# A group norm, weight split and bidirectional convolutional GRU on one core: the head rebuilt, and the split of the image spread over the first blocks

## The chip, the cores and the metric

The kernel runs on 1 core of one Trainium2 chip. The metric is the device time of one execution in microseconds (us). Engines are named as in the profile: PE (TensorE), PEld (its weight loads), DVE (VectorE), ACT (ScalarE), POOL (GpSimd), SP (SyncE, which here only issues DMAs).

## The reference

```python
xs_h = x.transpose(2, 0, 1, 3)                      # x is the group norm of the input, 8x128x32x32
def step(h, xr):                                     # once per row (or column) of the image
    xi = xr.transpose(0, 2, 1).reshape(b * L, c)
    out = _gru_step(xi, h, wih, whh)                 # r, z, n = sigmoid, sigmoid, tanh; (1 - z) * n + z * h
    ctx = out.reshape(b, L, c).transpose(0, 2, 1)
    h_new = jnp.tanh(_conv1d(ctx, cw, cb)).transpose(0, 2, 1).reshape(b * L, c)
    return (h_new, ctx)
...
ctx_above = _direction(xs_h, wih_d, whh_d, cw_d, cb_d).transpose(1, 2, 0, 3)
ctx_below = _direction(xs_h[::-1], wih_u, whh_u, cw_u, cb_u)[::-1].transpose(1, 2, 0, 3)
ctx_left = _direction(xs_w[::-1], wih_r, whh_r, cw_r, cb_r)[::-1].transpose(1, 2, 3, 0)
out = jnp.einsum('bchw,oc->bohw', context_map, w_comb) + b_comb[None, :, None, None]
```

The input is normalised over 32 groups of 4 channels, three recurrences of 32 steps run over it (rows downwards, rows upwards, columns from the right), and the combination of their contexts is added to the input.

## The kernel before, in words

Products are made in float16 pairs: a value is split in a HI part (float16 of the scaled value) and a LO part (what is left), and each product is three matmuls: weights HI by data HI, weights LO by data HI, weights HI by data LO. The scales of the weights are powers of two from the largest column sum of each of seven sets.

**The three directions** k = 0, 1, 2 each take 32 steps s. `blocks` issues 33 x 3 blocks (t, j). Block (t, j) works on direction j at step t (`now`), on the next direction (`nxt`) and on the one before (`before`). In a block PE does the nine matmuls of a convolution, nine of the hidden products and nine of the input products, 256 columns each. ACT does, in this order: the tanh of the new value (`new_value`, L419), the tanh of a convolution (`hidden`, L424), the sigmoid of both gates of the next direction (`gates`, L407), the HI parts of the context and of the hidden state (L430, L435) and, where j is 2, the copy of the next image column (`column`, L402). DVE does `blend` (L600, L608), `reset_hidden` (L615), `context_lo` (L620), `tanh_argument` (L627), `hidden_lo` (L632) and `z_times_h` (L638). An engine takes its instructions in the order in which they are written. t = 0, 1 and 31, 32 are written out, and between them runs a hardware loop of 29 turns.

**The head**, before the first block. SP loads the weights of three directions, the combination's weights, and then the eight images. ACT sums the weights' magnitudes (L335); POOL takes the maximum over the partitions (`partition_all_reduce`, L285); DVE makes the scales; ACT scales the weights in place (L342) and rounds them (L348); POOL subtracts for the LO parts (`weights_lo`, L299). DVE takes the statistics of each image (L489, L493); PE averages them over the groups in three batches of images (L682, L685); POOL raises to the power -1/2 (L292). ACT and DVE write normalised copies of the images into halves of the context stores that are still free (L354, L527). The copies are split in HI and LO image by image: edge rows and last columns first (L370 to L373 on ACT, L307 on POOL, L536 on DVE), the rest (L360 and L544) partly ahead of and partly in the blocks (0, 0) to (1, 0):

```python
REST_HI_IN_BLOCK = {(0, 0): (4,), (0, 1): (5, 6), (0, 2): (7,)}
REST_LO_AHEAD = 3
REST_LO_IN_BLOCK = {(0, 0): (3,), (0, 1): (4, 5), (0, 2): (6,), (1, 0): (7,)}
```

PE runs 8 products into a bank that nobody reads (L825, `WARM_PRODUCTS`), waits for all edge splits and begins with `input_products(0, 0)`.

Of the kernel before, what the change touches and what calls it, by code (L numbers as in the profile page):

```python
# [18 lines left out]
STEPS = H  # L19
COLS = B * LINE  # L20
PAD = LINE + 2
SPACE = H * W
# [18 lines left out]
BATCHES = ((0, 3), (3, 7), (7, 8))  # L41
ACT_IMAGES = (0, 1, 3)
DVE_IMAGES = (2, 4, 5, 6, 7)
POOL_IMAGES = 2
EDGE = 4
LAST_COLS = 2
WHOLE_IMAGES = 3
REST_HI_IN_BLOCK = {(0, 0): (4,), (0, 1): (5, 6), (0, 2): (7,)}
REST_LO_AHEAD = 3
REST_LO_IN_BLOCK = {(0, 0): (3,), (0, 1): (4, 5), (0, 2): (6,), (1, 0): (7,)}  # L50
WARM_PRODUCTS = 8


def build(nc, x_d, w_d, bias_d, out_d):
# [4 lines left out]
    with ExitStack() as ctx:  # L59
# [27 lines left out]
        allsum = sb("allsum", [C, SETS], f32)  # L87
# [4 lines left out]
        group_avg = sb("group_avg", [C, C], f32)  # L92
        stats = sb("stats", [C, B, CHUNKS_B, 6], f32)
# [5 lines left out]
        inv_std = sb("inv_std", [C, B], f32)  # L99
# [4 lines left out]
        def two_images(k, part):  # L104
            lines = slice(STEPS // 2, STEPS) if k == 0 else slice(0, STEPS // 2)
            return ctx_store[k][:, part, lines, :, :].rearrange("p t b l -> p (t b l)")[:, 0:4 * SPACE] \
                .bitcast(f32).rearrange("p (i h w) -> p i h w", i=2, h=H)

        x_norm = [two_images(k, part)[:, i, :, :] for k in (0, 2) for part in range(2) for i in range(2)]
# [3 lines left out]
        magnitudes = ctx_store[2][:].rearrange("p a t b l -> p (a t b l)")[:, 0:2 * BLOCKS * C] \  # L113
            .bitcast(f32).rearrange("p (n c) -> p n c", n=BLOCKS)
# [13 lines left out]
        avg_bank = [conv_bank[0], conv_bank[1], n_bank[2]]  # L128
# [8 lines left out]
        aggr_done = sem("aggr_done")  # L137
        mean_avg = sem("mean_avg")
# [9 lines left out]
        x_lo_pool = sem("x_lo_pool")  # L148
        x_lo_dve = sem("x_lo_dve")
        rest_hi_done = sem("rest_hi_done")  # L150
        rest_lo_done = sem("rest_lo_done")
        x_col_done = sem("x_col_done")
        sum_done = sem("sum_done")
        allsum_done = sem("allsum_done")
        scale_done = sem("scale_done")
        w_scaled = sem("w_scaled")
# [37 lines left out]
        def blocks(eng, block):  # L194

            for t in (0, 1):
                for j in range(DIRS):
                    block(t, j)
            with eng.Fori(2, STEPS - 1) as t:
# [24 lines left out]
        def gate_scale(k):  # L224
            return descale[:, k:k + 1]
# [6 lines left out]
        def conv_scale(k):  # L232
            return descale[:, DIRS + k:DIRS + k + 1]
# [3 lines left out]
        def edge_rows(ap):  # L237
            return ap.rearrange("p (g r) w -> p g r w", r=EDGE)[:, 0:H // EDGE:H // EDGE - 1, :, :]

        def last_columns(ap):  # L240
            return ap[:, EDGE:H - EDGE, W - LAST_COLS:W]

        def rest(ap):
            return ap[:, EDGE:H - EDGE, 0:W - LAST_COLS]
# [4 lines left out]
        def _(sp):  # L249

            for k in list(range(DIRS)) + [COMB]:
# [16 lines left out]
        def _(pool):  # L268
# [11 lines left out]
                                    channel_multiplier=-1).then_inc(pool_built, 1)  # L280
            for k in range(DIRS):
                nc.gpsimd.memset(context[k][:, :, 0:PAD:PAD - 1], 0.0).then_inc(sides_zero, 1)

            pool.wait_ge(sum_done, SETS)
            nc.gpsimd.partition_all_reduce(allsum[:], abs_sum[:], C, bass.bass_isa.ReduceOp.max) \  # L285
                .then_inc(allsum_done, 1)

# [604 lines left out]
```

## Time and profile before

| | before |
|---|---|
| median of 3 runs | 366.3 us (366.17 to 366.49) |
| the profiled execution, its own time | 366.35 us |
| its span in the trace | 364.6 us |
| busy: PE, DVE, ACT, POOL | 324.1 (89%), 308.2 (85%), 275.0 (75%), 15.8 (4%) us |
| chain that ended last | PE 85%, ACT 5%, DVE 4%, issue 2%, DMA 2%, POOL 1% |
| instructions | 7973 |
| read and written in device memory | 6.16 MB, 4.19 MB |

The span is what the trace covers; 1.75 us of the execution's time lie around it. The chain is what led to the last instruction, followed backwards. Busy time counts overlapping instructions once.

### The profile page before, as it was taken

Reading aid. Unit: us, or ns where it says so; the run is one execution under the profiler, and the core shown is the slowest. Engines: PE = TensorE matmul, PEld = TensorE weight load, DVE = VectorE, ACT = ScalarE, POOL = GpSimd, SP = SyncE. Lnnn points to the kernel's source line nnn. Section 1 sums busy time; section 2 is a strip of 40 time slices with the busy share of each in tenths; the row PEclk is TensorE's granted clock in tenths of the full one; section 3 lists DMA queues with packets and bytes.
Section 4 is the critical chain, followed back from the end, with each engine's and each line's share of the span. In section 5 each row is a group of like instructions: output and inputs, shape, how many; then the busy total and the mean of one; then the engine's idle time right before and its main releaser. Section 6 shows DMA issues by size and latency. Waiting matters only on the chain.

```text
span 364.6 us, 7973 instructions
## 1 busy us (share of the span) xinstructions
PE 324.1 (89%) x2702; PEld 261.3 (72%) x2702; DVE 308.2 (85%) x766; ACT 275.0 (75%) x573; POOL 15.8 (4%) x26
## 2 busy tenths in 40 slices
PE   0002798999999999999999999999999999999995
PEld 0002477888888888888888888888888888873442
DVE  0659989999998899999999999999899888987875
ACT  6538897888888888888888888888888888867400
POOL 1056101000000000000000000000000000000000
PEclk9999899999999999999999999999999999999999
DMA  7900000000000000000000000000000000000433
GB/s 301 375 0 1 1 2 0 2 0 0 0 0 0 0 0 0 0 0 0 0 0 0 0 0 0 0 0 0 0 0 0 0 0 0 0 0 36 174 138 115
DMA packets 4182, 10.43 MB, mean 29 GB/s; under 512 B 592, under 2 KB 720, under 8 KB 4176
## 3 DMA queue, kind: packets, MB, share of 16 engines
q1 hardware_dynamic: 4176, 10.36, 7.4%
q8 instruction: 3, 0.05, 0.1%
q14 instruction: 3, 0.02, 0.0%
HBM read 6.16 MB, written 4.19 MB: 28 GB/s over the span
## 4 chain that ended last, share of the span: by engine, by line
PE 85%; ACT 5%; DVE 4%; issue 2%; DMA 2%; POOL 1%; SPq 0%; ACTq 0%
PE rz_bank L690 22%; PE conv_bank L690 17%; PE rz_bank L693 11%; PE n_bank L690 11%; PE conv_bank L693 8%; PE n_bank L693 5%; DMA ctx_store<-weights_dram 2%; ACT ctx_store L342 1%; PE rz_bank L776 1%; PE n_bank L776 1%; PE rz_bank L780 1%; PE n_bank L780 1%; PE n_bank L778 1%; PE rz_bank L778 1%; DVE stats L489 1%
## 5 line engine op out<-in xcount | busy, mean ns | idle before, releaser
L690 PE MATMUL conv_bank<-ctx_store,w_parts 128*128 (+1 forms) x558 | 108.9, 275 | 1.4 <-ACT ctx_store L430 0.9
L690 PE MATMUL rz_bank<-h_parts,w_parts 128*128 128x256 f16 x372 | 76.2, 273 | 0.1
L407 ACT ACTIVATE rz<-rz_bank,descale 128x512 f32<-128x512 f32 x96 | 65.9, 686 | 7.9 <-PE rz_bank L690 2.4
L419 ACT ACTIVATE nval<-npre 128x256 f32<-128x256 f32 x93 | 38.4, 413 | 40.5 <-DVE npre L627 40.5
L693 PE MATMUL conv_bank<-ctx_store,w_parts 128*128 (+1 forms) x279 | 67.2, 275 | 0.0
L690 PEld LDWEIGHTS conv_bank<-ctx_store,w_parts 128*128 128x128 f16 x558 | 54.3, 98 | 17.2 <-ACT ctx_store L430 6.6
L615 DVE SCALAR_TENSOR_TENSOR npre<-n_bank,descale,rz 128x256 f32<-128x256 f32 x93 | 45.0, 484 | 24.5 <-ACT rz L407 24.3
L690 PE MATMUL rz_bank<-x_rows,w_parts 128*128 (+1 forms) x256 | 52.8, 274 | 2.0 <-issue 2.0
L424 ACT ACTIVATE hval<-conv_bank,biases,descale 128x256 f32<-128x256 f32 x93 | 52.0, 560 | 0.0
L693 PE MATMUL rz_bank<-h_parts,w_parts 128*128 128x256 f16 x186 | 45.7, 273 | 0.0
L690 PE MATMUL n_bank<-h_parts,w_parts 128*128 128x256 f16 x186 | 45.6, 273 | 0.0
L627 DVE SCALAR_TENSOR_TENSOR npre<-n_bank,descale,npre 128x256 f32<-128x256 f32 x93 | 44.5, 478 | 0.0
L620 DVE SCALAR_TENSOR_TENSOR ctx_store<-context,ctx_store 128x272 f32 (+1 forms) x96 | 41.8, 436 | 0.6 <-ACT ctx_store L430 0.5
L608 DVE TENSOR_TENSOR context<-rz,nval 128x256 f32<-128x256 f32 x93 | 39.5, 425 | 3.2
L600 DVE SCALAR_TENSOR_TENSOR nval<-rz,nval 128x256 f32<-128x256 f32 x96 | 40.5, 422 | 1.3 <-ACT nval L419 0.7
L430 ACT ACTIVATE ctx_store<-context 128x272 f32 (+1 forms) x96 | 40.6, 423 | 1.0 <-DVE context L608 1.0
L690 PEld LDWEIGHTS rz_bank<-h_parts,w_parts 128*128 128x128 f16 x372 | 36.3, 98 | 5.4 <-DVE h_parts L632 0.4
L632 DVE SCALAR_TENSOR_TENSOR h_parts<-hval,h_parts 128x256 f16<-128x256 f32 x93 | 39.0, 420 | 0.4 <-ACT h_parts L435 0.4
L638 DVE TENSOR_TENSOR rz<-rz,hval 128x256 f32<-128x256 f32 x93 | 39.0, 420 | 0.0
L435 ACT ACTIVATE h_parts<-hval 128x256 f16<-128x256 f32 x93 | 37.5, 403 | 0.1
L402 ACT ACTIVATE x_col<-x_rows 128x512 f16 (+1 forms) x32 | 34.8, 1088 | 1.2 <-DVE x_rows L536 1.2
L693 PE MATMUL rz_bank<-x_rows,w_parts 128*128 (+1 forms) x128 | 35.0, 274 | 0.0
(110 smaller groups left out, 499.6 us busy)
## 6 DMA issues: line engine op xcount, KB each, us to landing
x<-x_dram SPq DMA_DIRECT2D x8, 512.0 KB, 9.3
out_dram<-x_rows SPq DMA_DIRECT2D x16, 256.0 KB, 2.0
ctx_store<-weights_dram SPq DMA_DIRECT2D x3, 576.0 KB, 5.1
ctx_store<-weights_dram SPq DMA_DIRECT2D x1, 192.0 KB, 6.1
biases<-biases_dram SPq DMA_DIRECT2D x1, 2.0 KB, 11.6
```

The costliest lines, as they stand in the source:

```text
L407: nc.scalar.activation(rz[k][:].rearrange("p g c -> p (g c)"), rz_bank[k][:], ACT.Sigmoid, scale=gate_scale(k)).then_inc(sig_done[k], 1)
L424: nc.scalar.activation(hval[k][:], conv_bank[k % 2][:, 0:COLS], ACT.Tanh, bias=biases[:, k:k + 1], scale=conv_scale(k)).then_inc(h_done[k], 1)
L430: nc.scalar.activation(context_lines(k, s, HI), context[k][:].rearrange("p b l -> p (b l)"), ACT.Copy, scale=ACT_SCALE).then_inc(ctx_hi_do ...
L600: nc.vector.scalar_tensor_tensor(nval[k][:], z, 1.0, nval[k][:], ALU.subtract, ALU.mult).then_inc(zn_done[k], 1)
L608: nc.vector.tensor_tensor(out=context[k][:, :, 1:1 + LINE], in0=lines(zh), in1=lines(nval[k][:]), op=ALU.subtract).then_inc(ctx_done[k], 1)
L615: nc.vector.scalar_tensor_tensor(npre[k][:], n_bank[k][:, COLS:2 * COLS], gate_scale(k), rz[k][:, 0, :], ALU.mult, ALU.mult).then_inc(rh_d ...
L620: nc.vector.scalar_tensor_tensor(context_lines(k, s, LO), context[k][:].rearrange("p b l -> p (b l)"), ACT_SCALE, context_lines(k, s, HI), ...
L627: nc.vector.scalar_tensor_tensor(npre[k][:], n_bank[k][:, 0:COLS], gate_scale(k), npre[k][:], ALU.mult, ALU.add).then_inc(npre_done[k], 1)
L632: nc.vector.scalar_tensor_tensor(h_parts[k][:, LO, :], hval[k][:], ACT_SCALE, h_parts[k][:, HI, :], ALU.mult, ALU.subtract).then_inc(h_lo_ ...
L638: nc.vector.tensor_tensor(out=rz[k][:, 0, :], in0=rz[k][:, 1, :], in1=hval[k][:], op=ALU.mult)
L690: last = nc.tensor.matmul(out, w_block(HI, k, n), parts(hi_or_lo), start=start, stop=stop and hi_or_lo == LO, skip_group_check=True)
L693: last = nc.tensor.matmul(out, w_block(LO, k, n), parts(HI), start=False, stop=False, skip_group_check=True)
```

## The change

- SP loads the first direction's weights, then the eight images, then the other weights. Once all 19 splits of the image are made (`SPLITS`), it loads the eight images a second time, since they are now normalised in place and the sum at the end needs the input; ACT waits for that before the last additions.
- The maxima of the weight sums are taken by PE: one matmul turns the sums onto a few partitions (L729), DVE reduces, and a second matmul spreads the result (L735). It is done for the first two sets alone and later for the other five.
- ACT takes the mean and the variance of images 2 and 5 (L384 to L392), DVE those of six images. One average over the groups serves all images. POOL does the power once, and no other work beside the setting up of constants.
- ACT rounds and scales weights in one instruction (L398); DVE makes their LO parts in one (L580). It is done in ten units of three 128x128 blocks (`UNITS`), four of them ahead of the blocks.
- The image is normalised in its own place in three pieces: edge rows (2 + 2), a strip of 4 columns, and the core of 28x28. Core pieces stand in blocks (0, 1), (0, 2) and (1, 0), three on ACT, five on DVE.
- The split in HI (L412, ACT) and LO (L571, DVE) takes a strip of all eight images at once: two strips ahead of the blocks, 17 in blocks (0, 0) to (9, 2). `WAIT_SPLITS` names the blocks in which PE waits for every split of the blocks before.
- Blocks t = 0 to 10 are written out; the loop has 20 turns.
- PE has 12, 4, 4 and 6 products that nobody reads, between the small matmuls of the head.

```diff
+SPLIT_IN_BLOCK = {
+    (0, 0): LAST_COLS,
+    (1, 0): Cells((2, 4), (0, W - 4)),
+    (1, 1): Cells((H - 4, H - 2), (0, W - 4)),
+    (1, 2): Cells((4, 6), (0, W - 4)),
+    (2, 0): Cells((8, H - 8), (W - 8, W - 4)),
+    (2, 1): Cells((H - 6, H - 4), (0, W - 4)),
+    (2, 2): Cells((6, 8), (0, W - 4)),
+    (3, 0): Cells((H - 8, H - 6), (0, W - 4)),
+    (4, 0): Cells((8, 10), (0, W - 8)),
+    (4, 2): Cells((H - 10, H - 8), (0, W - 8)),
+    (5, 1): Cells((12, H - 12), (W - 12, W - 8)),
+    (6, 0): Cells((10, 12), (0, W - 8)),
+    (6, 2): Cells((H - 12, H - 10), (0, W - 8)),
+    (7, 2): Cells((12, 14), (0, W - 12)),
+    (8, 1): Cells((14, 16), (0, W - 12)),
+    (9, 0): Cells((16, 18), (0, W - 12)),
+    (9, 2): Cells((18, 20), (0, W - 12)),
+}
+WAIT_SPLITS = ((0, 0), (1, 2), (2, 0), (3, 2), (4, 0), (7, 2), (8, 0), (10, 1))
...
+def splits_before(t, j):
+
+    return 2 + sum(block < (t, j) for block in SPLIT_BLOCKS)
...
+UNITS_IN_BLOCK = {(0, 0): ("in 2", "conv 1"), (0, 1): ("rec 1",), (0, 2): ("conv 2",), (1, 0): ("rec 2",),
+                  (3, 1): ("comb",)}
+CORE_ON_ACT = {(0, 1): (5,), (0, 2): (6,), (1, 0): (7,)}
+CORE_ON_DVE = {(0, 1): (0, 1), (0, 2): (2, 3), (1, 0): (4,)}
...
+            load_weights(0)
             for b in range(B):
                 sp.dma_start(x32[:, b, :, :], x_d[b, :, :, :]).then_inc(x_loaded[b], 16)
+            for k in (1, 2, COMB):
+                load_weights(k)
             sp.dma_start(biases[:], bias_d).then_inc(bias_loaded, 16)
+
+            sp.wait_ge(x_lo_done, SPLITS)
+            for b in range(B):
+                sp.dma_start(x32[:, b, :, :], x_d[b, :, :, :]).then_inc(x_loaded[b], 16)
...
+            def image_moments(b):
+
+                i = ACT_IMAGES.index(b)
+                act.wait_ge(x_loaded[b], 16)
+                moment(nc.scalar.activation(summed[:, 2 * i, :, :], x32[:, b, :, :], ACT.Identity,
+                                            accum_out=image_sum[:, i:i + 1]))
...
+                moment(nc.scalar.activation(summed[:, 2 * i + 1, :, :], x32[:, b, :, :], ACT.Square,
+                                            bias=minus_mean[:, i:i + 1], accum_out=square_sum[:, i:i + 1]))
...
+            def x_hi(cells, normed):
+
+                act.wait_ge(x_normed, normed * (B - len(ACT_NORMED)))
+                act.wait_ge(x_normed_act, normed * len(ACT_NORMED))
+                nc.scalar.activation(all_images(x_rows[:, HI, :, :, :], cells),
+                                     x32[:, :, cells.rows, cells.cols], ACT.Copy).then_inc(x_hi_done, 1)
+
+            magnitude_sums(0)
+            image_moments(ACT_IMAGES[0])
+            for unit in range(3):
+                weights_hi(unit)
+            image_moments(ACT_IMAGES[1])
+            for k in (1, 2, COMB):
+                magnitude_sums(k)
+            for b in ACT_NORMED:
+                normalise(b, edges)
+            x_hi(FIRST_ROWS, 1)
+            x_hi(LAST_ROWS, 1)
+            for b in ACT_NORMED:
+                normalise(b, strip)
+            weights_hi(UNITS.index("in 1"))
...
+                    for unit in UNITS_IN_BLOCK.get((t, j), ()):
+                        weights_hi(UNITS.index(unit))
+                    for b in CORE_ON_ACT.get((t, j), ()):
+                        normalise(b, core)
+                    if (t, j) in SPLIT_IN_BLOCK:
+                        x_hi(SPLIT_IN_BLOCK[t, j], 2 if t == 0 else 3)
...
+                if isinstance(t, int) and (t, j) == (0, 0):
+                    act.wait_ge(x_lo_done, splits_before(0, 1))
+                    column(0)
...
+            def x_lo(cells):
+
+                lo_count[0] += 1
+                dve.wait_ge(x_hi_done, lo_count[0])
+                nc.vector.tensor_tensor(out=all_images(x_rows[:, LO, :, :, :], cells),
+                                        in0=x32[:, :, cells.rows, cells.cols],
+                                        in1=all_images(x_rows[:, HI, :, :, :], cells),
+                                        op=ALU.subtract).then_inc(x_lo_done, 1)
...
+            image_stats(0)
+            sets_peak(0)
+            image_stats(1)
+            weight_scales(0)
+            image_stats(3)
+            image_stats(4)
+            weights_lo(0)
+            weights_lo(1)
+            image_stats(6)
+            image_stats(7)
+            spread()
+            weights_lo(2)
+            variance()
+            shift()
+            for b in dve_normed:
+                normalise(b, edges)
+            sets_peak(1)
+            x_lo(FIRST_ROWS)
+            weight_scales(1)
+            x_lo(LAST_ROWS)
+            for b in dve_normed:
+                normalise(b, strip)
+            weights_lo(UNITS.index("in 1"))
...
+            pe.wait_ge(pool_built, 6)
+            turn_sums(0)
+            spread_peaks(0)
+            pe.wait_ge(w_hi_done, 2)
+            warm(FRONT_WARM)
+            pe.wait_ge(aggr_done, B - len(ACT_IMAGES))
+            pe.wait_ge(act_stats, 2 * len(ACT_IMAGES))
+            nc.tensor.matmul(avg_bank[:, 0:B], group_avg[:], meanvar[:, :, 0],
+                             start=True, stop=True).then_inc(mean_avg, 1)
+            warm(CHAIN_WARM)
+            pe.wait_ge(spread_done, 1)
+            nc.tensor.matmul(var_bank[:, 0:B], group_avg[:], dev[:],
+                             start=True, stop=True).then_inc(var_avg, 1)
+            warm(CHAIN_WARM)
+            turn_sums(1)
+            spread_peaks(1)
+            warm(LAST_WARM)
...
                 k, s = lagged(t, j, -1)
+                if isinstance(t, int) and t < UNROLLED and (t, j) in WAIT_SPLITS:
+
+                    pe.wait_ge(x_lo_done, splits_before(t, j))
```

ACT in the blocks (0, 0) and (0, 1), before. Each row is an instruction with its tiles and the semaphores it waits for; `x_rows<-ctx_store` is a rest of an image being rounded.

```order
43 L407 ACTIVATE rz<-rz_bank,descale 128x512 [waits rz_ready_1]
44 L360 ACTIVATE x_rows<-ctx_store 128x24x30
45 L430 ACTIVATE ctx_store<-context 128x272 [waits ctx_done_0]
46 L415 ACTIVATE nval<-n_bank,descale 128x256 [waits n_ready_1]
47 L407 ACTIVATE rz<-rz_bank,descale 128x512 [waits rz_ready_2]
48 L360 ACTIVATE x_rows<-ctx_store 128x24x30 x2
```

The same place now: the first column (`x_col`) is no longer copied ahead of the blocks.

```order
27 L440 ACTIVATE rz_1<-rz_bank_1,descale 128x512 [waits rz_ready_1]
28 L398 ACTIVATE w_parts<-ctx_store_1,w_scale 128x384 [waits scale_done] x2
29 L412 ACTIVATE x_rows<-x32 128x8x28x4 [waits x_normed_act,x_normed]
30 L463 ACTIVATE ctx_store_0<-context_0 128x272 [waits ctx_done_0]
31 L435 ACTIVATE x_col<-x_rows 128x512 [waits x_lo_done]
32 L448 ACTIVATE nval_1<-n_bank_1,descale 128x256 [waits n_ready_1]
33 L440 ACTIVATE rz_2<-rz_bank_2,descale 128x512 [waits rz_ready_2]
34 L398 ACTIVATE w_parts<-ctx_store_1,w_scale 128x384 [waits scale_done]
35 L404 ACTIVATE x32<-x32,x_shift,x_scale 128x28x28 [waits x_factor]
```

Behind the sigmoid of direction 1 there stand now two units of weights and the split of the last columns; the column's copy waits for DVE's half of that split.

DVE in block (1, 1), before, where the block holds no extra work:

```order
92 L600 SCALAR_TENSOR_TENSOR nval<-rz,nval 128x256 [waits n_done_1]
93 L608 TENSOR_TENSOR context<-rz,nval 128x8x32 [waits zn_done_1]
94 L615 SCALAR_TENSOR_TENSOR npre<-n_bank,descale,rz 128x256 [waits n_ready_2,sig_done_2]
95 L620 SCALAR_TENSOR_TENSOR ctx_store<-context,ctx_store 128x272 [waits ctx_hi_done_1]
96 L627 SCALAR_TENSOR_TENSOR npre<-n_bank,descale,npre 128x256 [waits rh_done_2]
```

The same block now:

```order
74 L642 SCALAR_TENSOR_TENSOR nval_1<-rz_1,nval_1 128x256 [waits n_done_1]
75 L650 TENSOR_TENSOR context_1<-rz_1,nval_1 128x8x32 [waits zn_done_1]
76 L657 SCALAR_TENSOR_TENSOR npre_2<-n_bank_2,descale,rz_2 128x256 [waits n_ready_2,sig_done_2]
77 L571 TENSOR_TENSOR x_rows<-x32,x_rows 128x8x2x28 [waits x_hi_done]
78 L662 SCALAR_TENSOR_TENSOR ctx_store_1<-context_1,ctx_store_1 128x272 [waits ctx_hi_done_1]
79 L669 SCALAR_TENSOR_TENSOR npre_2<-n_bank_2,descale,npre_2 128x256 [waits rh_done_2]
```

A split stands between the reset gate's product and the LO part of the context, and all that follows on DVE is queued behind it.

PE at the input products of block (1, 2), now (before, the same row waited for `rest_lo_done`):

```order
115 L765 MATMUL rz_bank<-h_parts,w_parts 128x256
116 L765 MATMUL n_bank<-h_parts,w_parts 128x256
117 L768 MATMUL n_bank<-h_parts,w_parts 128x256
118 L765 MATMUL n_bank<-h_parts,w_parts 128x256
119 L765 MATMUL rz_bank<-x_rows,w_parts 128x256 [waits sig_done_0,x_lo_done]
```

The input products of direction 0 wait here for the split of the block before; blocks (2, 0) and (8, 0) have such a row too.

## Rows read from the trace of the kernel before

**Rows 1.** First line of the page.

```profile
span 364.6 us, 7973 instructions
```

**Rows 2.** Timeline of the head: start, us, engine, line, operation, tiles [idle before <-releaser].

```profile
4.89 0.84 ACT L335 ACTIVATE ctx_store<-ctx_store 128x768 f32<-128x768 f32 x1 [2.61 <-DMA ctx_store<-weights_dram]
...
15.43 1.23 DVE L489 BATCH_NORM_STATS2 stats<-x 128x6 f32<-128x512 f32 x2
...
34.14 1.12 POOL L292 TENSOR_TENSOR inv_std<-gvar,minus_half 128x4 f32<-128x4 f32 x1 [0.61 <-DVE gvar L511]
...
35.96 3.50 PE L825 MATMUL rz_bank<-w_parts 128*128 128x512 f16 x8
...
41.42 0.27 PE L690 MATMUL rz_bank<-x_rows,w_parts 128*128 128x256 f16 x1 [1.96 <-issue]
```

**Rows 3.** Windows: us, PE, PEld, DVE, ACT, POOL busy (x), PEclk, DMA share, GB/s.

```profile
14.00:16.00 2.00, 0.00 (x0) 0.00 (x0) 1.97 (x6) 1.89 (x3) 0.00 (x0) 1.00 1.05 420
...
43.00:44.00 1.00, 1.00 (x6) 0.75 (x5) 1.00 (x2) 0.87 (x3) 0.00 (x0) 0.50 0.00 0
...
120.00:129.00 9.00, 9.00 (x84) 7.79 (x82) 8.12 (x22) 7.55 (x17) 0.00 (x0) 1.00 0.00 0
```

**Rows 4.** Timeline of ACT: the sigmoids of the gates in the first blocks.

```profile
43.66 0.69 ACT L407 ACTIVATE rz<-rz_bank,descale 128x512 f32<-128x512 f32 x1
...
45.62 0.68 ACT L407 ACTIVATE rz<-rz_bank,descale 128x512 f32<-128x512 f32 x1
...
49.92 0.69 ACT L407 ACTIVATE rz<-rz_bank,descale 128x512 f32<-128x512 f32 x1 [0.66 <-PE rz_bank L690]
...
54.19 0.67 ACT L407 ACTIVATE rz<-rz_bank,descale 128x512 f32<-128x512 f32 x1
...
58.08 0.69 ACT L407 ACTIVATE rz<-rz_bank,descale 128x512 f32<-128x512 f32 x1 [0.24 <-PE rz_bank L690]
...
61.11 0.69 ACT L407 ACTIVATE rz<-rz_bank,descale 128x512 f32<-128x512 f32 x1
...
64.08 0.69 ACT L407 ACTIVATE rz<-rz_bank,descale 128x512 f32<-128x512 f32 x1
```

**Rows 5.** Timeline of ACT in a block with a column, in the loop.

```profile
123.83 0.69 ACT L407 ACTIVATE rz<-rz_bank,descale 128x512 f32<-128x512 f32 x1
124.41 0.42 ACT L430 ACTIVATE ctx_store<-context 128x272 f32 x1
124.73 0.41 ACT L435 ACTIVATE h_parts<-hval 128x256 f16<-128x256 f32 x1
125.04 1.09 ACT L402 ACTIVATE x_col<-x_rows 128x512 f16 x1
126.04 0.40 ACT L419 ACTIVATE nval<-npre 128x256 f32<-128x256 f32 x1
126.34 0.54 ACT L424 ACTIVATE hval<-conv_bank,biases,descale 128x256 f32<-128x256 f32 x1
```

**Rows 6.** Timeline of DVE in the same block.

```profile
124.55 0.48 DVE L615 SCALAR_TENSOR_TENSOR npre<-n_bank,descale,rz 128x256 f32<-128x256 f32 x1 [0.28 <-ACT rz L407]
124.95 0.43 DVE L620 SCALAR_TENSOR_TENSOR ctx_store<-context,ctx_store 128x272 f32 x1
125.30 0.48 DVE L627 SCALAR_TENSOR_TENSOR npre<-n_bank,descale,npre 128x256 f32<-128x256 f32 x1
```

**Rows 7.** Groups of 0 to 58 us, shapes apart: count | busy, mean ns | idle before.

```profile
L544 DVE TENSOR_TENSOR x_rows<-ctx_store,x_rows 128x720 f16<-128x720 f32 x8 | 7.0, 900 | 0.0
...
L360 ACT ACTIVATE x_rows<-ctx_store 128x720 f16<-128x720 f32 x5 | 3.9, 797 | 0.0
...
L354 ACT ACTIVATE ctx_store<-x,x_shift,x_scale 128x1024 f32<-128x1024 f32 x3 | 3.7, 1236 | 7.9 <-DVE x_shift L523 7.9
L342 ACT ACTIVATE ctx_store<-ctx_store,w_scale 128x384 f32<-128x384 f32 x4 | 2.4, 600 | 0.0
...
L536 DVE TENSOR_TENSOR x_rows<-ctx_store,x_rows 128x256 f16<-128x256 f32 x6 | 2.5, 417 | 0.0
```

More of the change, by code:

```diff
@@ L92, in build @@
         group_avg = sb("group_avg", [C, C], f32)
+        unit_diag = sb("unit_diag", [C, C], f32)
+        ones = sb("ones", [SETS, C], f32)
+        peak = [sb(f"peak_{n}", [SETS, 1], f32) for n in range(2)]
+        peak_diag = [sb(f"peak_diag_{n}", [SETS, SETS], f32) for n in range(2)]
+        image_sum = sb("image_sum", [C, len(ACT_IMAGES)], f32)
+        minus_mean = sb("minus_mean", [C, len(ACT_IMAGES)], f32)
+        square_sum = sb("square_sum", [C, len(ACT_IMAGES)], f32)
         stats = sb("stats", [C, B, CHUNKS_B, 6], f32)
@@ L194, in blocks @@
         def blocks(eng, block):
-            for t in (0, 1):
+            for t in range(UNROLLED):
                 for j in range(DIRS):
                     block(t, j)
-            with eng.Fori(2, STEPS - 1) as t:
+            with eng.Fori(UNROLLED, STEPS - 1) as t:
                 for j in range(DIRS):
@@ L232, in conv_scale, with edges, strip, core @@
         def conv_scale(k):
[L233 to L244, printed above, removed]
+            return descale[:, 2 * k + 1:2 * k + 2]
+        def edges(ap):
+            return ap.rearrange("p (g r) w -> p g (r w)", r=2)[:, 0:H // 2:H // 2 - 1, :]
+        def strip(ap):
+            return ap[:, LAST_COLS.rows, LAST_COLS.cols]
+        def core(ap):
+            return ap[:, LAST_COLS.rows, 0:LAST_COLS.cols.start]
+        def all_images(ap, cells):
+            return ap[:, cells.rows, :, cells.cols].rearrange("p h b w -> p b h w")
+        def unit_blocks(unit):
+            kind, *k = UNITS[unit].split()
+            if kind == "comb":
+                return COMB_SET, 0, DIRS
+            k = int(k[0])
+            first = DIRS + k * DIR_BLOCKS + GATES * ("in", "rec", "conv").index(kind)
+            return 2 * k + (kind == "conv"), first, first + GATES
+        def merged(ap):
+            return ap.rearrange("p n c -> p (n c)")
         block = ctx.enter_context(nc.Block())
@@ L249, in _, with load_weights @@
         def _(sp):
-            for k in list(range(DIRS)) + [COMB]:
+            def load_weights(k):
                 lo, hi = (DIRS + k * DIR_BLOCKS, DIRS + (k + 1) * DIR_BLOCKS) if k != COMB else (0, DIRS)
@@ L560, in _ @@
+            dve_normed = [b for b in range(B) if b not in ACT_NORMED]
             image_stats(0)
-            weight_scales()
+            sets_peak(0)
             image_stats(1)
-            image_stats(2)
-            spread(0)
+            weight_scales(0)
             image_stats(3)
-            variance(0)
             image_stats(4)
-            factor(0)
-            shift(0)
-            image_stats(5)
+            weights_lo(0)
+            weights_lo(1)
             image_stats(6)
-            normalise(2)
@@ L649, in steps @@
                 if exists(now[1]):
[L650 to L651 removed]
+                    if isinstance(t, int):
+                        for unit in UNITS_IN_BLOCK.get((t, j), ()):
+                            weights_lo(UNITS.index(unit))
+                        for b in CORE_ON_DVE.get((t, j), ()):
+                            normalise(b, core)
+                        if (t, j) in SPLIT_IN_BLOCK:
+                            x_lo(SPLIT_IN_BLOCK[t, j])
                     context_lo(*now)
@@ new lines, in spread_peaks, with warm @@
+            def spread_peaks(n):
+                first, end = SET_GROUPS[n]
+                pe.wait_ge(peak_done, n + 1)
+                nc.tensor.matmul(peak_bank[n][:, C:C + end - first], ones[0:end - first, :],
+                                 peak_diag[n][0:end - first, 0:end - first], start=True, stop=True) \
+                    .then_inc(peak_spread, 1)
+            def warm(products):
+                for _ in range(products):
+                    nc.tensor.matmul(rz_bank[2][:], w_block(HI, 0, 0),
+                                     merged(w_parts[:, HI, DIRS:DIRS + OUT_COLS // C, :]),
+                                     start=True, stop=True, skip_group_check=True)
```

318 lines of the change are left out of this document (124 added, 194 removed).

## The prediction

> **What bounds the kernel now.** I read three things in this order: the windows, to see what a block in the loop costs and which engine fills it; the timeline of the head, to see when the first real matmul can run; and the sigmoids of the gates on ACT as milestones, since each block has exactly one.
>
> In the loop PE is busy 9.00 us of 9.00 and makes three blocks in that time [rows 3]. A block's 27 matmuls therefore last 2.98 us, and ACT and DVE must fit in between. They do so narrowly. From one sigmoid (call its start 0) ACT goes 0.58 to the context's HI part, 0.90, 1.21 to the column, 2.21 to the tanh, 2.51 to the next tanh [rows 5], and the next sigmoid can start 0.46 later: at 2.97, exactly PE's period. Without the column it is bound by DVE instead: the reset product at 0.72, context LO at 1.12, tanh argument at 1.47, done at 1.95 [rows 6], then 0.33 and 0.46 on ACT: 2.77, so 0.2 us of slack. **The loop has nearly no room for extra work.** The span runs 41.42 us without a real matmul [rows 2], and the first blocks, which hold the rest of the split, take 4.30, 4.27 and 3.89 us instead of 3 (differences of neighbours from 45.62 to 58.08, [rows 4]). What the change can win is in that head; what it can lose is in the blocks.
>
> **The new head, step by step.** Weights 0 land at 4.89 as before [rows 2]. An image of 0.52 MB takes 1.25 us at 420 GB/s [rows 3]: image 0 lands at about 6.1, image 2 at 8.7, image 7 at 14.9, the last weights at 18.2.
> - DVE: six images of statistics, 1.45 each (two halves 1.23 [rows 2] and some 0.2 for the aggregation), 8.7; scales and peaks of two sets about 1.2; two LO units at 0.55 each (384 elements, between 0.42 and 0.90 [rows 7]). From 6.1 that ends at 17.2.
> - ACT: image 2 from 8.7, two passes of about 1.3 and three tiny instructions, 3.2; three units at 0.51 (0.60 less the overlap [rows 7]); image 5, 3.2: 16.7. The sums of the other weights last until 20.1, behind the chain.
> - Chain: mean matmul 0.6 to 17.9, three small DVE steps to 18.45, warm products, second average to 19.2, power 1.12 [rows 2] to 20.6, shift 20.85, edges of five images 21.7, HI of the first rows 22.3, LO 23.0. PE then still has six warm products: 1.3 us at the full clock, 2.6 at half. The eight products of before took 3.50 us [rows 2], 0.43 for 512 columns, which is the 1.2 GHz level. So the first real matmul comes at 23.9 to 25.1 instead of 41.42.
> - Direction 1 must wait for the unit "in 1", the last item of DVE's list, at 25.9. Its sigmoid comes at 26.95, against 43.66 [rows 4]: **minus 16.7**. POOL's subtractions and the three-batch chain vanish here, with no successor on the path.
>
> **The first blocks, sigmoid to sigmoid.** Prices: a split of 448 elements costs ACT 0.57 (between 272 elements at 0.42 [rows 5] and 720 at 0.797 [rows 7]) and DVE 0.62 (between 0.417 and 0.900 [rows 7]), 0.53 as a step in DVE's queue. A core of 784 costs ACT 0.97 (below 1.236 for 1024 [rows 7]) and DVE 0.62 as a step, my estimate; bounds 0.42 and 0.90.
> - (0, 0): two units 1.02, last columns 0.93, then DVE's LO 1.0, then the column 1.09, which is now ahead of direction 2's first product, then 1.05 on PE: 0.58+1.02+0.93+1.07+1.1+1.05 = 5.75, against 1.96: **plus 3.8**.
> - (0, 1): ACT adds 1.48 where two rests took 1.4 before: 4.5, **plus 0.2**. (0, 2): adds 1.48 where 0.7 stood: 5.05, **plus 0.8**.
> - (1, 0): unit, core and split are in series, and the split on ACT must wait for DVE's last core, which waits for ACT's unit: LO ends at 3.63, then 0.35+0.51+0.33+0.46: 5.3 against 3.89, **plus 1.4**.
> - PE blocks (1, 2) and (2, 0) wait for the split of the block just before, though the line they read was ready earlier. That split ends at 1.16+0.60 = 1.76; then nine input products 0.97, nine of the convolution 1.0, and the first of the hidden ones 0.68: 4.45. Against 3.03 and 2.97 [rows 4] that is **plus 1.4 and plus 1.5**.
>
> **The spread splits.** With a split in it, a block's chain is: ACT to 1.13, DVE starts at 1.16, 0.53, then 0.35+0.51+0.33+0.46 = 3.34 instead of 2.97, plus 0.37. With a column ACT needs 3.44, plus 0.47. In a lone split PE keeps part of its lead, and it costs what the context's HI part is late, 0.13 to 0.23. Four splits in a run, (2, 0) to (3, 0), make 1.7, the unit "comb" 0.43, the eight singles 0.07 to 0.22 each 1.3; block (8, 0) waits as (2, 0) does, 1.2. **Plus 4.6** in all. Below, a split can cost nothing (all slack in the next block), above, both its steps in full, 1.0.
>
> **The loop.** Nine turns fewer. Two neighbouring periods are 3.03 and 2.97 [rows 4], so a turn's end costs 0.06: **minus 0.5**. The Trainium skill (Runtime: NRT & Kernel Launch, Instruction fetch mechanics) says that a taken branch leaves the sequential prefetch and can stall on a fetch; the trace shows only those 0.06 us, and by a full stall a turn the gain would be larger.
>
> **The clock.** PE's granted clock was 0.50 in 43 to 44 us [rows 3], after PE had stood idle 1.96 us before its first real product [rows 2], and only six matmuls started in that microsecond, where the loop starts 84 in 9 us [rows 3]. In the new start-up PE idles 4.6 us behind block (0, 0), so I expect the same once or twice and take **plus 1.2** (bounds 0 and 7.2, below).
>
> **The tail.** The images loaded again, 4.2 MB, take 10 us at 420 GB/s [rows 3] from about 115 us on and are needed at 325: nothing. If that cover went, ACT would wait those 10 us at the end. The tail is the same.
>
> Sum: -16.7+3.8+0.2+0.8+1.4+1.4+1.5+4.6-0.5+1.2 = **-2.3 us**. The profiled execution took 366.35 us with a span of 364.6 [rows 1], and stands 0.05 above the median: 364.05, so **364.0 us**. Most of 16.7 us of gain is given back later.
>
> **Rivals.**
> - **The clock stays low (slower).** At the 1.2 GHz level 27 products take 5.75 us. Were it low through the start-up, the three middle blocks would grow by 1.25, 0.7 and 0.45, and the two that wait (24 products 5.1, behind the split's 1.76) by 2.4 each: 7.2, less the 1.2 counted: 370.0 us. It decides once the low stretch costs more than 3.5 us. For it: PE will be busy only 60% of a start-up block. Against: at the low clock PE is filled, and after such a stretch the clock came back, since the loop runs 84 products in 9 us [rows 3]. The Trainium skill (TensorE: Matmul & The Clock Gate, The HAM clock gate) has throttled as the default state and activity as what releases it, which makes this rival possible by rule.
> - **Splits cost both steps in full (slower).** 14 extras at 0.8 instead of a mean of 0.24: plus 7.8, 371.8 us. For it: DVE has 0.9 us free in 9 [rows 3]. Against: the chain above has room.
> - **The head is not as short.** The one average waits for the last of eight images and for both ACT images; a hidden wait among the many semaphore hops, or direction 1's unit, may cost 3 us: 367 us.
> - **The blocks absorb it (faster still).** DVE is ahead in the waited-for splits (minus 3.5), lone splits free (minus 1.2), no clock loss (minus 1.2): 358.1 us.
>
> **How the numbers follow.** Forecast, within 2 us of 364.0: 0.55. Absorbed: 0.18. Head longer: 0.12. Clock: 0.09. Full price: 0.06. A measurement of this kernel tells 0.2%, 0.7 us, from no change. Faster: 0.53 from the forecast, 0.18 from absorbed and 0.01 from the long head, 0.72. Same: 0.02 from the forecast, 0.04 from the long head, 0.06. Slower: 0.07 from the long head and both dear cases, 0.22. The range leaves out the two dear cases and the end of the cheap one: 358.5 to 368.5 us.
>
> **What would show it.** The first input product at 24 to 25 us; gaps between the sigmoids of 5.7, 4.5, 5.0, 5.3, 4.4, 4.4; PE in the windows from 55 to 100 us busy less than 9 of 9, with periods of 3.2 to 3.5 in blocks with a split and 4.2 before (8, 0); the granted clock at 0.5 somewhere between 25 and 40 us. I am wrong if the first product comes after 28 us, if blocks with a split have a period of 2.98, or if the low clock lasts over 8 us.

## The result and the profile after

The changed kernel took 369.2 us (median of 20 runs, 367.4 to 371.0), the kernel before 367.1 us in the same comparison (20 runs, 366.1 to 368.2). The ratio is 1.0054, with a 95% interval of 1.0034 to 1.0074: **0.5% slower**, where 364.0 us and faster was forecast. Half of the changed kernel's runs lie between 367.4 and 368.4 us and half between 370.0 and 371.0, so that the median stands in the gap, where no run is; what parts them comes below. The profiled execution is of the lower half (367.5 us). In it the change costs 1.2 us of span against [rows 1].

The head of the page after, and its rows of busy time and granted clock:

```profile
span 365.8 us, 7776 instructions
...
PE 330.9 (90%) x2720; PEld 260.7 (71%) x2720; DVE 309.7 (85%) x772; ACT 277.8 (76%) x590; POOL 4.2 (1%) x16
...
PEclk9988999999999999999999999999999999999999
```

There are 197 instructions fewer, and the span is no shorter for it. Of 40 slices two have a clock digit of 8 (18 to 37 us). The timeline of the head after answers to [rows 2]:

```profile
5.41 0.84 ACT L377 ACTIVATE ctx_store<-ctx_store 128x768 f32<-128x768 f32 x1 [3.11 <-DMA ctx_store<-weights_dram]
...
23.17 2.74 PE L741 MATMUL rz_bank<-w_parts 128*128 128x512 f16 x6
25.70 0.42 PE L765 MATMUL rz_bank<-x_rows,w_parts 128*128 128x256 f16 x1
```

The first real matmul starts at 25.70 us instead of 41.42. **The head is 15.7 us shorter, nearly all that was claimed for it.** The gates' sigmoids on ACT, the milestones of [rows 4], show where it goes:

```profile
27.91 0.69 ACT L440 ACTIVATE rz<-rz_bank,descale 128x512 f32<-128x512 f32 x1
33.94 0.69 ACT L440 ACTIVATE rz<-rz_bank,descale 128x512 f32<-128x512 f32 x1 [0.92 <-PE rz_bank L765]
39.27 0.69 ACT L440 ACTIVATE rz<-rz_bank,descale 128x512 f32<-128x512 f32 x1 [1.40 <-PE rz_bank L765]
44.26 0.68 ACT L440 ACTIVATE rz<-rz_bank,descale 128x512 f32<-128x512 f32 x1
49.56 0.69 ACT L440 ACTIVATE rz<-rz_bank,descale 128x512 f32<-128x512 f32 x1
54.28 0.69 ACT L440 ACTIVATE rz<-rz_bank,descale 128x512 f32<-128x512 f32 x1
59.00 0.69 ACT L440 ACTIVATE rz<-rz_bank,descale 128x512 f32<-128x512 f32 x1
62.54 0.69 ACT L440 ACTIVATE rz<-rz_bank,descale 128x512 f32<-128x512 f32 x1
```

Call direction 1's first sigmoid number 1; number 3t+j+1 is the one that PE's block (t, j) leads to, and ACT's block (t, j) runs from there to the next. Number 1 is 15.75 us earlier than before (27.91 against 43.66, [rows 4]), number 7 only 5.08 (59.00 against 64.08), number 24 still 1.20 (113.67 against 114.87). Number 25 is 0.34 late, behind PE's wait in block (8, 0), and from number 32 on the changed kernel is 1.1 to 1.2 us late, until the end. The forecast had minus 16.7, then minus 6.4, then minus 2.3.

The two periods of 4.72 (to 54.28 and 59.00) are the waits for a split just before, as forecast. The timelines of DVE and PE after show the second:

```profile
55.46 0.62 DVE L571 TENSOR_TENSOR x_rows<-x,x_rows 128x448 f16<-128x448 f32 x1
...
56.15 0.28 PE L765 MATMUL rz_bank<-x_rows,w_parts 128*128 128x256 f16 x1 [1.58 <-DVE x_rows L571]
```

PE stood 1.58 us for the LO half of rows that its block does not read. A block with one split in the loop's steady part is the next loss. ACT's and DVE's timelines after, block (4, 0), where a split of 384 elements stands alone:

```profile
79.25 0.68 ACT L440 ACTIVATE rz<-rz_bank,descale 128x512 f32<-128x512 f32 x1
79.83 0.52 ACT L412 ACTIVATE x_rows<-x 128x384 f16<-128x384 f32 x1
80.24 0.42 ACT L463 ACTIVATE ctx_store<-context 128x272 f16<-128x272 f32 x1
...
82.58 0.69 ACT L440 ACTIVATE rz<-rz_bank,descale 128x512 f32<-128x512 f32 x1
```

```profile
79.96 0.48 DVE L657 SCALAR_TENSOR_TENSOR npre<-n_bank,descale,rz 128x256 f32<-128x256 f32 x1
80.38 0.56 DVE L571 TENSOR_TENSOR x_rows<-x,x_rows 128x384 f16<-128x384 f32 x1
80.85 0.44 DVE L662 SCALAR_TENSOR_TENSOR ctx_store<-context,ctx_store 128x272 f16<-128x272 f32 x1
81.20 0.48 DVE L669 SCALAR_TENSOR_TENSOR npre<-n_bank,descale,npre 128x256 f32<-128x256 f32 x1
81.60 0.41 DVE L674 SCALAR_TENSOR_TENSOR h_parts<-hval,h_parts 128x256 f16<-128x256 f32 x1
```

The period is 3.33 us instead of 2.97. PE's timeline has one gap in it:

```profile
80.22 0.27 PE L765 MATMUL n_bank<-x_col,w_parts 128*128 128x256 f16 x1
80.72 0.28 PE L765 MATMUL conv_bank<-ctx_store,w_parts 128*128 128x256 f16 x1 [0.22 <-ACT ctx_store L463]
...
82.17 0.38 PE L765 MATMUL rz_bank<-h_parts,w_parts 128*128 128x256 f16 x2
```

Neighbouring products start 0.11 us apart, so the convolution's turn was at 80.33, and it starts 0.39 late, when the context's HI part (L463) is done. That part stands behind ACT's half of the split, a step of 0.41 (79.83 to 80.24). In the kernel before, it was done at 121.86 and the convolution started at 121.97, in its turn: after a hop of 0.06 as here (80.66 to 80.72) PE had some 0.05 us of lead, and nearly the whole step reaches the period. Behind the gap PE runs without another one to the products that release the sigmoid at 82.58.

DVE is close behind. Its half takes 0.47 us of its queue (80.38 to 80.85), and everything behind it is late by that: the context's LO part, and `hidden_lo` (L674), which the last two products of the gates read. It ends at 82.01 and they start at 82.17, so here they don't wait. In the kernel before, it ended 2.28 us after the start of the sigmoid before it (120.86) and they started 2.55 after it; now it ends 2.76 after it: had ACT's half cost nothing, this path would still have made the block about 0.27 longer (an estimate from these times and the hop of 0.06).

PE was busy 8.71 of 9 us between 120 and 129, against 9.00 before [rows 3], since splits still stand there. The images' second load, whose cover the forecast named, cost nothing; PE is full while it runs:

```profile
140.00:144.00 4.00, 4.00 (x38) 3.47 (x37) 3.44 (x9) 3.23 (x8) 0.00 (x0) 1.00 1.02 398
```

### The profile page after: what moved, and what is told of

The parts are those of the page before. It is cut to its first block, busy times and chain, and to the rows that moved or that the text cites. A ratio compares the mean times of both kernels' runs of the same rounds, so it can differ in the third digit from the quotient of the medians.

```text
span 365.8 us, 7776 instructions
## 1 busy us (share of the span) xinstructions
PE 330.9 (90%) x2720; PEld 260.7 (71%) x2720; DVE 309.7 (85%) x772; ACT 277.8 (76%) x590; POOL 4.2 (1%) x16
## 4 chain that ended last, share of the span: by engine, by line
PE 75%; ACT 12%; issue 6%; DVE 5%; POOL 1%; POOLq 0%; ACTq 0%
PE rz_bank L765 19%; PE conv_bank L765 16%; PE rz_bank L768 9%; PE n_bank L765 9%; PE conv_bank L768 8%; PE n_bank L768 4%; ACT rz L440 3%; ACT x_col L435 2%; ACT x_rows L412 2%; DVE x_rows L571 1%; ACT hval L457 1%; ACT ctx_store L463 1%; PE rz_bank L851 1%; ACT nval L452 1%; DVE npre L657 1%
## 5 line engine op out<-in xcount | busy, mean ns | idle before, releaser
L463 ACT ACTIVATE ctx_store<-context 128x272 f32 (+1 forms) x96 | 40.5, 422 | 1.0 <-DVE context L650 1.0
L674 DVE SCALAR_TENSOR_TENSOR h_parts<-hval,h_parts 128x256 f16<-128x256 f32 x93 | 38.5, 414 | 0.2 <-ACT h_parts L468 0.2
```

The source lines that it names most:

```text
L463: nc.scalar.activation(context_lines(k, s, HI), context[k][:].rearrange("p b l -> p (b l)"), ACT.Copy, scale=ACT_SCALE).then_inc(ctx_hi_do ...
```

## Experiments

Every comparison is with the kernel before, on the same chip. Its median there was 367.7 us. A period is read from one profiled execution of each kernel.

**Wait only for what is read.** In the three places PE waits for one split fewer.

```diff
-pe.wait_ge(x_lo_done, splits_before(t, j))
+pe.wait_ge(x_lo_done, splits_before(t, j) - ((t, j) in ((1, 2), (2, 0), (8, 0))))
```

> Edit: in blocks (1, 2), (2, 0) and (8, 0) PE waits for one split fewer, so not for the split of the block just before, which the products there do not read. Theory A (the wait is on the path): the periods before the three following sigmoids, 4.72, 4.72 and 4.51 us in the changed kernel, fall to what ACT and DVE need with a split, 3.4 to 3.5; the kernel gets 3.5 to 4 us faster than the changed one, about 365.3 us. Theory B (ACT and DVE bound these blocks anyway): less than 1 us.

Measured: 364.25 us (6 runs, 363.0 to 367.0), ratio 0.9921, interval 0.9892 to 0.9951. ACT's timeline in this kernel:

```profile
52.81 0.69 ACT L440 ACTIVATE rz<-rz_bank,descale 128x512 f32<-128x512 f32 x1 [0.71 <-PE rz_bank L765]
56.23 0.69 ACT L440 ACTIVATE rz<-rz_bank,descale 128x512 f32<-128x512 f32 x1
59.65 0.69 ACT L440 ACTIVATE rz<-rz_bank,descale 128x512 f32<-128x512 f32 x1
```

The two periods fall from 4.72 to 3.42, that of (8, 0) from 4.51 to 3.32: 3.8 us together. **The over-strict waits alone turn the sign of the change**: without them it is faster than the kernel before. Two of the six runs, the profiled one with them, are near 367 us and four at 363.0 to 364.6.

**Idle products against the low clock.** On the changed kernel, ten products with no use behind direction 1's first input products, to keep PE from standing idle in block (0, 0).

```diff
                 if exists(s):
                     input_products(k, s)
+                if isinstance(t, int) and (t, j) == (0, 0):
+                    warm(10)
```

> Edit: ten products of 512 columns that nobody reads behind the input products of direction 1, in PE's idle stretch of 4.6 us before the first column. Theory A (the low clock behind the stretch costs time): granted clock stays at the 2.4 GHz level from 28 to 38 us, the next two periods, 6.03 and 5.33 us, fall by 0.3 and 0.7 us, in all 1 us faster than the changed kernel, and its runs scatter less than 367.4 to 371. Theory B (the clock falls elsewhere, or falls harmlessly): within 0.3 us, same scatter.

Measured: 368.6 us (7 runs, 366.9 to 369.4), ratio 1.0033, interval 1.0011 to 1.0054. The period to number 2 fell by 0.28 and that to number 3 rose by 0.3 against the first profile; in four profiles of the unchanged kernel they are 5.92 to 6.38 and 5.33 to 6.12. The granted clock was 0.50 in 34 to 36 us all the same and low again from 46 to 52, with a period of 6.81. The means of preventing it failed here, so this run says nothing on what the low clock costs.

**The split at the end of its block.** The first experiment, and from the second step on both halves of a split stand last in their block: on ACT behind `hidden_hi`, on DVE behind `z_times_h`.

```diff
+                if isinstance(t, int) and t > 0 and (t, j) in SPLIT_IN_BLOCK:
+                    x_hi(SPLIT_IN_BLOCK[t, j], 3)
...
                     z_times_h(nxt[0])
+                if isinstance(t, int) and t > 0 and (t, j) in SPLIT_IN_BLOCK:
+                    x_lo(SPLIT_IN_BLOCK[t, j])
```

> Edit: as e1, and from block (1, 0) on the split stands at the end of the block on both engines: on ACT behind the hidden state's HI part, where ACT idles 0.6 us in a block without a column, on DVE behind z times h. Theory A (a split costs 0.3 to 0.45 us each because it stands between the sigmoid and the context, ahead of the tanh argument): blocks with a split and no column fall from 3.25-3.45 to 3.0-3.15 us, those with a column stay at 3.4; 2 to 3 us faster than e1, about 363 us. Theory B (DVE has no room at all, whatever the place): same as e1 within 0.5 us.

Measured: 363.3 us (5 runs), ratio 0.988, interval 0.9858 to 0.9903. About 1 us better than the first experiment, not 2 to 3. The period to number 5, of block (1, 0), falls from 5.30 in the changed kernel's first profile to 4.36, which is nearly all of it; the lone splits still cost 0.23 to 0.41 each. DVE's and ACT's timelines around the split of block (4, 0) say why:

```profile
78.96 0.55 DVE L573 TENSOR_TENSOR x_rows<-x,x_rows 128x384 f16<-128x384 f32 x1
79.43 0.42 DVE L644 SCALAR_TENSOR_TENSOR nval<-rz,nval 128x256 f32<-128x256 f32 x1
79.88 0.43 DVE L652 TENSOR_TENSOR context<-rz,nval 128x256 f32<-128x256 f32 x1
```

```profile
80.34 0.43 ACT L463 ACTIVATE ctx_store<-context 128x272 f16<-128x272 f32 x1 [0.26 <-DVE context L652]
```

ACT's half is out of the way, but DVE's now stands ahead of the next blend (L644) and delays the next context. ACT stands 0.26 us for it, and PE 0.16 for the HI part behind that: the block lasts 3.29. The end of a block isn't where DVE has time.

**The split where DVE is idle.** In the kernel before DVE stands 0.28 us for ACT's sigmoid ahead of the reset product [rows 6]. ACT's half stays at the end of the block; DVE's goes to the next block, between the context (L652) and the reset product (L659). The table is spread anew, at most one split in two blocks where that can be, "comb" goes to block (6, 1), and each of PE's waits names the split that its line needs.

```diff
-    (4, 2): Cells((H - 10, H - 8), (0, W - 8)),
+    (5, 0): Cells((H - 10, H - 8), (0, W - 8)),
...
+WAIT_SPLITS = {(0, 0): 2, (1, 2): 4, (2, 0): 5, (3, 2): 6, (4, 0): 8, (7, 2): 11, (8, 0): 12, (10, 2): 19}
...
                     blend(*now)
+                    if isinstance(t, int) and (t, j) > (2, 0):
+                        last = (t, j - 1) if j else (t - 1, 2)
+                        if last in SPLIT_IN_BLOCK:
+                            x_lo(SPLIT_IN_BLOCK[last])
...
-                    pe.wait_ge(x_lo_done, splits_before(t, j) - ((t, j) in ((1, 2), (2, 0), (8, 0))))
+                    pe.wait_ge(x_lo_done, WAIT_SPLITS[t, j])
```

> Edit: on top of e3, from block (2, 0) on ACT's half of a split stands at the end of a block with j = 0 or 1 wherever the deadlines allow, and DVE's half in the next block between the context and the reset gate's product, where DVE idles 0.16 to 0.31 us until the sigmoid ends; the unit comb moves to (6, 1). PE waits for exactly the splits that its products read. Theory A (in e3 the split delays the blend and with it the context, since DVE leads by 0.15 us only there): a lone split now costs 0 to 0.1 us instead of 0.3, the kernel gets 2.5 to 3.5 us faster than e3, about 360.3 us. Theory B (DVE's total of 3.1 us a block is the bound): 0.2 us a split remains, at most 1 us faster than e3.

Measured: 359.8 us (6 runs), ratio 0.9784, interval 0.9758 to 0.981. The gates on ACT and DVE's queue around the split of block (4, 0):

```profile
75.14 0.69 ACT L440 ACTIVATE rz<-rz_bank,descale 128x512 f32<-128x512 f32 x1
...
76.42 0.51 ACT L412 ACTIVATE x_rows<-x 128x384 f16<-128x384 f32 x1
...
78.13 0.69 ACT L440 ACTIVATE rz<-rz_bank,descale 128x512 f32<-128x512 f32 x1
...
81.09 0.69 ACT L440 ACTIVATE rz<-rz_bank,descale 128x512 f32<-128x512 f32 x1
```

```profile
78.12 0.42 DVE L652 TENSOR_TENSOR context<-rz,nval 128x256 f32<-128x256 f32 x1
78.47 0.55 DVE L573 TENSOR_TENSOR x_rows<-x,x_rows 128x384 f16<-128x384 f32 x1
78.94 0.48 DVE L659 SCALAR_TENSOR_TENSOR npre<-n_bank,descale,rz 128x256 f32<-128x256 f32 x1
79.33 0.43 DVE L664 SCALAR_TENSOR_TENSOR ctx_store<-context,ctx_store 128x272 f16<-128x272 f32 x1
```

The periods are 2.99 and 2.96: the same 384 elements, and **a lone split costs nothing where both engines have time for it**, instead of 0.27 to 0.40. What was left: the run of splits in neighbouring blocks (periods of 3.48, 3.10, 3.13 and 3.14 to numbers 10 to 13), "comb" (3.45) and the last split, for which PE waits in block (10, 2) (3.75).

**The first block's columns first.** On that kernel, in block (0, 0) the split of the last columns goes ahead of the two weight units, on both engines.

```diff
+                    if (t, j) == (0, 0):
+                        x_hi(SPLIT_IN_BLOCK[t, j], 2)
                     for unit in UNITS_IN_BLOCK.get((t, j), ()):
                         weights_hi(UNITS.index(unit))
                     for b in CORE_ON_ACT.get((t, j), ()):
                         normalise(b, core)
-                    if (t, j) == (0, 0):
-                        x_hi(SPLIT_IN_BLOCK[t, j], 2)
```

> Edit: e5, and in block (0, 0) both engines do the split of the last columns ahead of the two units of weights, on which only later products wait. Theory A (the first column hangs on the chain units, split, LO, column): the third sigmoid comes 0.9 to 1.1 us earlier, period 5.0 instead of 6.0 to 6.4, and the kernel is 1 us faster than e5. Theory B (unit in 2, now later, holds the products of direction 2): less than 0.3 us.

Measured: 360.1 us (5 runs), ratio 0.9791, interval 0.9766 to 0.9816: no faster. The period to number 2 fell from 6.37 to 5.43 as expected, and that to number 3 rose from 5.66 to 6.16, where the granted clock is 0.50.

**The idle products again.** Six, on the kernel just described.

> Edit: e6 with six idle products of 512 columns behind direction 1's first input products. Theory A (clock): periods behind block (0, 0) shorter by 0.5 us and less scatter than e6. Theory B, from e2 where a low stretch came back later in 46 to 52 us: no faster than e6 within 0.3 us.

Measured: 358.2 us (5 runs), ratio 0.9758, interval 0.9734 to 0.9781. The window of 34 to 36 us in the changed kernel, and then in this one (columns as in [rows 3]):

```profile
34.00:36.00 2.00, 2.00 (x11) 1.40 (x10) 0.84 (x2) 2.00 (x4) 0.00 (x0) 0.50 0.00 0
```

```profile
34.00:36.00 2.00, 1.69 (x17) 1.28 (x15) 1.84 (x4) 1.97 (x5) 0.00 (x0) 1.00 0.00 0
```

At the full clock PE starts 17 products there instead of 11, and has time over. The periods to number 2 and 3 are 4.81 and 4.65 instead of 5.43 and 6.16, 2.1 us together, and 1.8 us in the median (360.07 to 358.23). That is the price of the low stretch in this kernel, whose clock is at half from 32 to 38 us; the forecast's 1.2 was for one or two such stretches.

**The changed kernel again, three times.** To see where its scatter comes from, it ran ten times more, and twice by itself.

> The changed kernel unchanged, for a second profile of it and beside the others on one chip. If its 370 us runs come from a second low stretch of PE's clock, a profile of such a run shows 0.5 in 46 to 53 us and one period of 6.8 us where the first profile has 5.30; a profile of a 367.5 us run repeats the first.

> The changed kernel again, one look. If the execution takes 370 us, a second stretch of the granted clock at 0.5 between 46 and 53 us and one period of about 6.8 us instead of 5.30 (as in the profiles of e1 and e2); if 367.5 us, the rows of the first profile again.

> As c1: one more look at the changed kernel, for an execution of the other kind.

Measured: 367.9 us (10 runs, 367.0 to 370.2; ratio 1.002, interval 0.9999 to 1.0041), and 367.8 and 370.7 us in the single runs. Beside the first comparison (1.0054) this is nearer to no change, since eight of these ten runs fell in the lower group; both stand. The window of 50 to 52 us in the run of 367.8 us, then in that of 370.7 us:

```profile
50.00:52.00 2.00, 0.42 (x5) 0.23 (x4) 1.85 (x6) 1.66 (x4) 0.00 (x0) 1.00 0.00 0
```

```profile
50.00:52.00 2.00, 2.00 (x11) 1.43 (x10) 1.81 (x5) 0.92 (x2) 0.00 (x0) 0.50 0.00 0
```

and ACT's timeline in the slower one:

```profile
45.94 0.68 ACT L440 ACTIVATE rz<-rz_bank,descale 128x512 f32<-128x512 f32 x1
52.77 0.69 ACT L440 ACTIVATE rz<-rz_bank,descale 128x512 f32<-128x512 f32 x1 [0.72 <-PE rz_bank L765]
```

The same program has a second low stretch in one execution and not in the other: the period is 6.83 us instead of 5.30. PE had stood 2.48 us ahead of that stretch in both. With a later start (number 1 at 28.46 against 27.91), a longer first stretch (1.1 us more to number 3) and the second (1.5) number 5 comes 3.2 us later than in the first profile, and the two runs are 3.2 us apart. That a granted clock at half in 48 to 54 us goes with the upper group rests on this run and on the first experiment's profile, which has it too (0.50 in 50 to 52) and was of a run of 367.0 us, nearly 3 above that kernel's median; the three profiles of lower runs (367.1, 367.5, 367.8 us) have 1.00 there.

**All together.** The last split one block earlier, "comb" in the slack places too.

```diff
-    (10, 0): Cells((18, 20), (0, W - 12)),
+    (9, 1): Cells((18, 20), (0, W - 12)),
...
+                if isinstance(t, int) and (t, j) == (6, 1):
+                    weights_hi(UNITS.index("comb"))
...
+                    if isinstance(t, int) and (t, j) == (6, 2):
+                        weights_lo(UNITS.index("comb"))
```

> Edit: e7, with the last split moved from (10, 0) to (9, 1), so that PE in (10, 2) doesn't wait for the split of the block before, and both halves of the unit comb put in the same places as the splits. Theory A (that wait and comb's place are what is left in the rows: one period of 3.76 us at the loop's entry and one of 3.45): both become 2.97 to 3.0, and the kernel gets 1.2 us faster than e7, about 357.0 us. Theory B: the 3.76 is the loop's entry itself; then only 0.4 us.

Measured: **356.8 us** (5 runs, 355.7 to 357.7), ratio 0.9714, interval 0.9687 to 0.9741. Its window from 120 to 129 us, first that of the changed kernel:

```profile
120.00:129.00 9.00, 8.71 (x79) 7.25 (x77) 8.23 (x23) 7.99 (x18) 0.00 (x0) 1.00 0.01 2
```

```profile
120.00:129.00 9.00, 9.00 (x85) 7.87 (x83) 8.70 (x24) 7.80 (x18) 0.00 (x0) 1.00 0.50 188
```

PE is full again, while the images' second load takes half of the DMA engines. The periods of "comb" (3.45) and of the last split (3.76) are gone. It has the changed kernel's head, and its work in another order (and six idle products more), and is 11 to 12 us faster.

What the splits cost was read from periods; no kernel without late splits was measured.

## Why the prediction was wrong

Its mechanisms were there, and its sum was small: 16.7 us of gain against 14.4 of loss. Errors of a few tenths in many terms and of 1.5 us in one, nearly all in one direction, were enough to turn the sign. In the order of its sum, from the changed kernel's profile:

| term | forecast | measured |
|---|---|---|
| head, to number 1 | -16.7 | -15.75 |
| (0, 0) | +3.8 | +4.07 |
| (0, 1) | +0.2 | +1.03 |
| (0, 2) | +0.8 | +0.72 |
| (1, 0) | +1.4 | +1.41 |
| PE (1, 2) and (2, 0), waiting | +1.4, +1.5 | +1.69, +1.75 |
| run of four splits | +1.7 | +1.91 |
| "comb" | +0.43 | +0.48 |
| lone splits, eight | +1.3 | +2.8 |
| PE (8, 0), waiting | +1.2 | +1.54 |
| loop turns | -0.5 | -0.5 |
| clock | +1.2 | in the rows above |

(Down to the waits of (1, 2) and (2, 0) each is a period after less the period before; below them, a period after less 2.97. The loop's is what remains of number 7 to number 32, 6.22 us, without the others.)

- **The step that failed** is the price of the lone splits: "In a lone split PE keeps part of its lead", 0.07 to 0.22 each. They cost 0.27 to 0.40 each, 2.8 us for eight instead of 1.3. The path was right, "what the context's HI part is late", and its size wrong: the HI part is late by ACT's whole step, 0.41 for 384 elements, and PE's lead over it is 0.05 us, not the 0.2 or so that the price implies. I also left out that DVE's queue has one order: with `hidden_lo` behind the split it is a second path, nearly as long. The term of the plain chain in the same paragraph, plus 0.37, was near the price of every one of them (0.35 in the mean). In the third experiment ACT's half is out of the way and DVE's still holds the block; in the fourth the same work has a place with time on both engines and costs nothing.
- **The head** was 0.95 short. The first weights were being read at 5.41 instead of 4.89, but the images' shift came on time (20.83 against 20.85). Behind it DVE's list was slower than added up: its edges ended at 22.27 against 21.7, and the unit "in 1", which number 1 waits for, at 26.81 against 25.9. The six idle products ran at half the clock (granted clock 0.50 in 23 to 25 us; 2.74 us for six, the dearer of the two ends given), and PE came to direction 1's products at 27.01, only some 0.1 behind what the unit allowed. The forecast had called the pace of the eight old products, 0.43 each, the 1.2 GHz level, while the granted clock of that stretch reads 1.00 (36 to 39 us of the kernel before); what slowed them is open.
- **The low clock** came where it was forecast, after PE had stood 4.6 us behind block (0, 0). It lies in the rows of (0, 0) and (0, 1), where it accounts for much of the surplus of 0.27 and 0.83 over the forecast: at the full clock (sixth experiment) the period of (0, 1) is 4.65 against the 4.5 forecast, here it is 5.33. In this profile that is no more than the 1.2 taken, but in the sixth experiment removing it gave 1.8 to 2.1 us. What the forecast had not at all is the second stretch, in half of the runs: 1.5 us there, of the 2.6 that lie between the middles of the two groups.
- **The waits** of (1, 2), (2, 0) and (8, 0) were right in kind and 0.25 to 0.34 low each, 4.98 together against 4.1. The first experiment gives 3.8 us for them, as it leaves the split itself in the blocks.
- Nothing was paid for the images' second load, and the turns gave their 0.5, both as forecast.
- Of the rivals, "The clock stays low" had part of the cause of the runs of 370 to 371 us, though it is a second stretch and not one that lasts. "Splits cost both steps in full" was too dear: 0.35, not 0.8. The range ended at 368.5, which held the lower half of the runs and missed the median.

The arithmetic of the whole: minus 6.4 to number 7 became minus 5.08, plus 4.1 from there became plus 6.22; that is 3.4 of the 5.2 us between 364.0 and 369.2, and the rest is the two groups, as the profiled run (367.5) was of the lower. Against the kernel before it is plus 2.1 instead of minus 2.3, since that kernel's own median was 367.1 here and not 366.3.

## What to carry to other kernels

In a loop with no slack the question isn't how much time an engine has over, it is where in its order that time lies: read what each instruction behind an inserted one releases, and put late work where the engine stands waiting for another anyway. The same split cost 0.36 us where it stood ahead of the context's HI part on ACT and behind the reset product on DVE, and nothing at the end of ACT's block and ahead of the reset product. Freeing one engine isn't enough: in the third experiment DVE's half held the block with ACT's out of the way. A wait on a counter should name the item that is read, not the last one issued; here that alone was worth 1%.

## What the hardware showed

- **In this start-up with gaps the clock differs from one execution to the next.** The same program had a further stretch at a granted clock of 0.50 in one execution and not in another, though PE had stood 2.48 us ahead of it in both, and its runs fell into two groups (middles at 367.6 and 370.2 us); the kernel before spread by 2.0 us without such groups. The Trainium skill (TensorE: Matmul & The Clock Gate, The HAM clock gate) says that the count of matmuls at the low clock changes from run to run of one kernel. The two single runs agree: 5 matmuls started in 50 to 52 us at a granted clock of 1.00 in one, 11 at 0.50 in the other.
- **Filling a gap with idle products removed the low stretch in one kernel and not in the other.** Ten products in the changed kernel gained nothing (clock at 0.50 in 34 to 36 us, and low again from 46); six in a kernel whose block (0, 0) was shorter kept the clock at 1.00 in 34 to 36 us and gave 1.8 us. PE stood 2.45 us behind the ten and 2.37 behind the six. Why six did what ten did not was not settled: the two kernels differ in more than the count.
- **The start-up's own idle products ran at the low clock.** PE was busy only 0.38 of the 2 us before 22 us; from 23 to 25 us the granted clock is 0.50 and the six products take 2.74 us, 0.46 each for 512 columns, where the loop's 27 of 256 columns take 2.98. They held the first real product back (25.70, while the LO part that it waits for ended at 23.74) instead of readying the clock for it.
